# Expert weights of a mixture layer picked from SBUF by registers instead of gathered from memory

## The reference

```python
x = x + _layernorm(_L0_attn_ref(_layernorm(x), ...))   # windowed attention, a recurrence over the tokens
x = x + _layernorm(_L0_ffn_ref(_layernorm(x), ...))    # the second layer
```

```python
attn = softmax(rope(q) @ rope(k).T / sqrt(8)); x1 = layernorm(x + (attn @ v) @ Wo + bo)
gate_probs = softmax(x1 @ Wg + bg)
topk_p, topk_i = top_k(gate_probs, 2); topk_p = topk_p / sum(topk_p)
h = gelu(einsum('bsd,edf->bsef', x1, W1) + b1)         # exact gelu
y = einsum('bsef,efd->bsed', h, W2) + b2
out = layernorm(x1 + einsum('bse,bsed->bsd', comb, y))  # comb: topk_p at the two experts, 0 elsewhere
```

## Time and profile before

| | |
|---|---|
| median of 3 runs (lowest to highest) | 3049.6 us (3047.81 to 3052.29) |
| the profiled execution: its time | 3038.8 us |
| its span, first to last instruction | 3037.1 us |
| PE busy (share) | 1260.7 us (42%) |
| PEld | 573.8 us (19%) |
| DVE | 2243.1 us (74%) |
| ACT | 1239.5 us (41%) |
| POOL | 380.9 us (13%), 495 instructions |
| mean granted TensorE clock | 0.664 of full speed |
| moved by DMA | 104.36 MB, 42.48 of them by the software queue (GpSimd's) |

### The profile page before, as it was taken

How to read it: one execution, slowest core, us unless ns; L and a number is a source line. 1 busy time by engine, 2 the same in 40 slices (tenths; PEclk the granted TensorE clock), 3 DMA queues, 4 the chain that set the end, 5 groups by cost and what they waited for, 6 DMA issues and landing times. The chain is left out here.

```text
span 3037.1 us, 37267 instructions
## 1 busy us (share of the span) xinstructions
PE 1260.7 (42%) x7320; PEld 573.8 (19%) x7320; DVE 2243.1 (74%) x15166; ACT 1239.5 (41%) x3176; POOL 380.9 (13%) x495
## 2 busy tenths in 40 slices
PE   2101101001001001010148785877758777578687
PEld 1000000000000000000011122333213322134255
DVE  6999999999999999998669973645655456554232
ACT  2333333333333333333515652555535554455532
POOL 0000000000000000000101104222043120312111
PEclk8555555555555555555569985878769787688788
DMA  4000000000000000000340202142122321222200
GB/s 100 1 1 1 1 1 1 1 1 1 1 1 1 1 1 1 1 1 3 70 90 18 64 18 76 46 125 61 27 84 75 106 52 21 84 70 66 83 15 8
DMA packets 91680, 104.36 MB, mean 34 GB/s; under 512 B 10350, under 2 KB 66456, under 8 KB 91448
## 3 DMA queue, kind: packets, MB, share of 16 engines
q1 hardware_dynamic: 77336, 59.49, 7.9%
q0 software_dynamic: 14112, 42.48, 4.6%
HBM read 73.04 MB, written 30.67 MB: 34 GB/s over the span
## 5 line engine op out<-in xcount | busy, mean ns | idle before, releaser
L1269 DVE TENSOR_REDUCE nm_half<-pair 128x2 f32<-128x1024 f32 x512 | 618.1, 1221 | 374.0 <-PE pair L1519 268.0
L1166 ACT ACTIVATE pt<-pair 128x1024 f32<-128x1024 f32 x512 | 512.5, 1024 | 523.7 <-PE pair L1529 424.1
L207 ACT ACTIVATE ex<-row,nmax 128x65 f32<-128x65 f32 x960 | 336.0, 350 | 923.5 <-DVE nmax L309 837.8
L267 DVE SCALAR_TENSOR_TENSOR junk<-ex,tab 128x65 f32<-128x65 f32 x2850 | 620.6, 219 | 1.4 <-issue 0.2
L370 PE MATMUL p_s<-tab,bdg 128*128 128x32 f32 x120 | 31.8, 406 | 829.7 <-DVE tab L272 829.7
L1495 PE MATMUL p_o<-pt,va 128*9 128x512 f32 x2048 | 312.1, 683 | 11.1 <-DVE o_sb L1298 5.3
L1519 PE MATMUL pair<-ks,qs 48*128 48x512 bf16 x1024 | 226.5, 440 | 179.1 <-ACT pt L1166 113.8
L272 DVE TENSOR_TENSOR tab<-raw,rz 128x1 f32<-128x1 f32 (+1 forms) x1890 | 285.8, 151 | 3.2 <-issue 1.1
L301 DVE SCALAR_TENSOR_TENSOR junk<-ex,rz,row 128x65 f32<-128x65 f32 x930 | 265.3, 285 | 3.0 <-issue 2.7
L1529 PE MATMUL pair<-qs,ks 50*128 50x512 bf16 x1024 | 223.4, 435 | 62.6 <-DVE nm_half L1269 34.7
L267 DVE DVE_READ_ACCUMULATOR junk<-ex,tab 128x1 f32 x2850 | 235.0, 82 | 0.3
(11 more groups left out here) (257 smaller groups left out, 2049.9 us busy)
## 6 DMA issues: line engine op xcount, KB each, us to landing
parts_dram<-parts SPq DMA_DIRECT2D x48, 256.0 KB
qs<-parts_dram SPq DMA_DIRECT2D x32, 192.0 KB, 4.7
ks<-parts_dram SPq DMA_DIRECT2D x32, 192.0 KB, 5.3
hid<-xs_dram SPq DMA_DIRECT2D x15, 256.0 KB
ys_dram<-hid SPq DMA_DIRECT2D x15, 256.0 KB
h_dram<-f SPq DMA_DIRECT2D x20, 128.0 KB, 2.5
x<-in_x SPq DMA_DIRECT2D x4, 512.0 KB, 8.5
w_dram<-in_W SPq DMA_DIRECT2D x8, 256.0 KB
```

The source lines that it names most:

```text
L207: nc.scalar.activation(ex[:, r % 2, :], row[:, r % 2, 1:], ACT.Exp, bias=nmax[:, r % 2:r % 2 + 1], accum_out=z[:, r % 2:r % 2 + 1]).then_i ...
L267: nc.vector.scalar_tensor_tensor(junk[:, g, :], ex[:, k, :], 1.0, tab[:, g, r:r + ROW], ALU.mult, ALU.mult, accum_out=raw[:, g:g + 1]).the ...
L1166: nc.scalar.activation(pt[:, kt % 2, :, tokens(t)], pair[fill.pair][:, :, :], ACT.Exp, scale=SCALE).then_inc(s_exp, 1)
L1269: nc.vector.reduce_max(nm_half[:, t, hp % 2, :, q], pair[fill.pair][:, :, :], AX.X, negate=True)\
```

## The change

W1 and W2 are loaded once, whole, in the first layer, and stay in SBUF; the copy of W2 in DRAM, the gathers (WG) and the reload (WL) go. A new step WC, due five units ahead of a group, lets GpSimd read the expert of each tile into a register and copy that expert's W1 into `w1`, a single buffer of four tiles in the memory of `yg`. It waits until the first expert product has used the group before (for the first group: until B2 is done with that memory). At the start of a group TensorE reads the same numbers into registers of its own; the product by W2 takes its operand at an address made from the register. `sel`, `upper` and `ones` of the rank products become bf16 (they hold 0, 1 and sums that fit).

```diff
+    pairs += [(w["W1"][:, :, :], io["W1"].rearrange("e d f -> d e f"))]
+    pairs += [(w["W2"][:, e, :, :], io["W2"][e].rearrange("(c p) d -> p c d", p=P)) for e in range(E)]
...
-         (2, 1): [("WG", j) for j in range(SLOTS)], (7, 2): [("YG",)]}
+         (7, 2): [("YG",)]}
...
+            if u + 5 in GROUP_AT:
+                due.insert(0, ("WC", GROUP_AT.index(u + 5)))
             if u + 3 in GROUP_AT:
                 due.insert(0, ("XS", GROUP_AT.index(u + 3)))
-            if u - 4 in GROUP_AT:
-                g = GROUP_AT.index(u - 4) + 2
-                due += [("WG", j) for j in in_group(g)]
...
-            if last and (hp, kt) == (7, 4):
-                due.append(("WL",))
...
-        sel, pw = sb("sel", [P, QT, E]), sb("pw", [P, 2, QT, E])
+        sel, pw = sb("sel", [P, QT, E], BF16), sb("pw", [P, 2, QT, E])
-        upper, ones = sb("upper", [P, P]), sb("ones_pp", [P, P])
+        upper, ones = sb("upper", [P, P], BF16), sb("ones_pp", [P, P], BF16)
...
+        w1 = yg[:, :, :, :].rearrange("p k q d -> p (k q d)").rearrange("p (j i) -> p j i", j=GROUP)
...
+                elif name == "WC":
+                    g = x[1]
+                    pool.wait_ge(s_experts, s)
+                    pool.sem_inc(s_pace_pool, 1)
+                    if g == 0:
+                        taken(pool, at["B2", 1])
+                        pool.sem_inc(s_pace_pool, 1)
+                    else:
+                        pool.wait_ge(s_hs, 2 * NG * (s - 1) + 2 * g)
+                        pool.sem_inc(s_pace_pool, 1)
+                    for j in in_group(g):
+                        e = pool.value_load(expert_u[0:1, j:j + 1], min_val=0, max_val=E - 1)
+                        nc.gpsimd.tensor_copy(w1[:, j % GROUP, :], w["W1"][:, bass.ds(e, 1), :].rearrange("p e i -> p (e i)"))\
+                            .then_inc(s_w1, 1)
...
-                    then(nc.vector.tensor_scalar(row_f[:, :], expert_t[:, :], float(P), parted[:, :], ALU.mult, ALU.add))
+                    nc.vector.tensor_copy(expert_u[:, :], expert_t[:, :]).then_inc(s_experts, 1)
...
                     g = tiles[0] // GROUP
+                    if x[1] % 2 == 0:
+                        pe.wait_ge(s_experts, s)
+                        for j in in_group(g):
+                            chosen[j] = pe.value_load(expert_u[0:1, j:j + 1], min_val=0, max_val=E - 1)
                     taken(pe, at["XS", g])
+                    pe.wait_ge(s_w1, NT * (s - 1) + tiles[-1] + 1)
                     emptied(s, fill)
                     for j in tiles:
-                        pe.wait_ge(s_wg[j % SLOTS], fetches(s, j))
                         for f in range(FC):
-                            ins = nc.tensor.matmul(pair[fill.pair][:, j % 2, tile(f)], w["W1"][:, j % SLOTS, tile(f)],
+                            ins = nc.tensor.matmul(pair[fill.pair][:, j % 2, tile(f)],
+                                                   w1[:, j % GROUP, tile(f)],
                                                    xst[:, g % 2, tile(j % GROUP)], start=True, stop=True)
...
-                                               w["W2"][:, j % SLOTS, f, :], start=f == 0, stop=f == FC - 1)
+                                               w["W2"][:, bass.ds(chosen[j], 1), f, :].rearrange("p e d -> p (e d)"), start=f == 0, stop=f == FC - 1)
```

More of the change, by code:

```diff
@@ L32 @@
 NG = -(-NT // GROUP)
-SLOTS = 2 * GROUP
 SCALE = 1.0 / float(np.sqrt(HD))
@@ L128, in _ @@
             loaded = load_constants(sp, w, io, s_weights)
[L130 to L133, removed]
+            xs_dram, _ = moe_dram
             sp.wait_ge(s_stacks, 2)
@@ L140, in _ @@
                              stacks["ones"][:, :].unsqueeze(1).broadcast_to((2, HP, T))).then_inc(s_weights, 16)
-            sp.wait_ge(s_weights, loaded + 32 + 16 * (E + 1))
+            sp.wait_ge(s_weights, loaded + 32 + 16)
         @block.gpsimd
@@ L858, in second_layer @@
         xr, xa2, acc = sb("xr", [P, QT, D]), sb("xa", [P, 2, QT, D]), sb("acc", [P, QT, D])
-        sel, pw = sb("sel", [P, QT, E]), sb("pw", [P, 2, QT, E])
+        sel, pw = sb("sel", [P, QT, E], BF16), sb("pw", [P, 2, QT, E])
         wk = sb("wk", [P, 2, 2, QT])
-        upper, ones = sb("upper", [P, P]), sb("ones_pp", [P, P])
-        lower, steps8, tiles_at, parted = sb("lower", [P, E, E]), sb("steps8", [P, QT]), sb("tiles_at", [P, NT]), sb("parted", [P, 1])
+        upper, ones = sb("upper", [P, P], BF16), sb("ones_pp", [P, P], BF16)
+        lower, steps8, tiles_at = sb("lower", [P, E, E]), sb("steps8", [P, QT]), sb("tiles_at", [P, NT])
         cmp8, tiles_of, upto, base = sb("cmp8", [P, E, E]), sb("tiles_of", [P, E]), sb("upto", [P, E]), sb("base", [P, E])
@@ L866, in second_layer @@
         before_t, expert_t = sb("before_t", [P, NT, E]), sb("expert_t", [P, NT])
-        row_f, row_u = sb("row_f", [P, NT]), sb("row_u", [P, NT], U32)
+        row_f, expert_u = sb("row_f", [P, NT]), sb("expert_u", [P, NT], U32)
         bias_t = sb("bias_t", [P, NT, FC])
         yg = sb("yg", [P, 2, QT, D])
+        w1 = yg[:, :, :, :].rearrange("p k q d -> p (k q d)").rearrange("p (j i) -> p j i", j=GROUP)
         part = yg[:, 0, :, :].rearrange("p (t q) d -> p t q d", t=2)
@@ L880, in second_layer @@
         hq = hq.rearrange("p (q d) -> p q d", q=QT)
-        xs_dram, ys_dram, w2_dram = moe_dram
+        xs_dram, ys_dram = moe_dram
         xt = aot
@@ L913, in second_layer @@
             sem(n) for n in ("s_gate", "s_gexp", "s_comb", "s_sum", "s_added", "s_fin", "s_out"))
-        s_sel, s_place, s_slots, s_rows, s_bias = (
-            sem(n) for n in ("s_sel", "s_place", "s_slots", "s_rows", "s_bias"))
-        s_sent, s_fetched, s_mixed, s_dense = sem("s_sent"), sem("s_fetched"), sem("s_mixed"), sem("s_dense")
+        s_sel, s_place, s_slots, s_experts, s_bias = (
+            sem(n) for n in ("s_sel", "s_place", "s_slots", "s_experts", "s_bias"))
+        s_sent, s_fetched, s_mixed = sem("s_sent"), sem("s_fetched"), sem("s_mixed")
         s_xs, s_ys = [sem(f"s_xs{i}") for i in range(2)], [sem(f"s_ys{i}") for i in range(2)]
-        s_wg = [sem(f"s_wg{i}") for i in range(SLOTS)]
+        s_w1 = sem("s_w1")
         s_hs, s_gs = sem("s_hs"), sem("s_gs")
@@ L938, in norm_index @@
             return NORMS.index((s, k))
-        def fetches(s, j):
-            return 32 * (len(range(j % SLOTS, NT, SLOTS)) * (s - 1) + j // SLOTS + 1)
         def group_loads(s, g):
@@ L1057, in step @@
                         .then_inc(s_ys[g % 2], 16)
[L1058 to L1063, removed]
             passes(sp, step)
@@ L1075, in _ @@
                            allow_small_or_imprecise_dtypes=True).then_inc(s_iota, 1)
-            nc.gpsimd.iota(parted[:, :], [[1, 1]], base=0, channel_multiplier=1,
-                           allow_small_or_imprecise_dtypes=True).then_inc(s_iota, 1)
             nc.gpsimd.memset(ones[:, :], 1.0).then_inc(s_iota, 1)
@@ L1080, in _ @@
             nc.gpsimd.memset(lower[:, :, :], 1.0).then_inc(s_iota, 1)
-            pool.wait_ge(s_iota, 7)
+            pool.wait_ge(s_iota, 6)
             nc.gpsimd.affine_select(out=upper[:, :], in_=upper[:, :], compare_op=ALU.is_ge, fill=0.0, base=-1,
@@ L1119, in step @@
                                 half_of(xa2, s)[:, q, :], None).then_inc(s_sent, 16)
[L1120 to L1125, removed]
-                        pool.sem_inc(s_pace_pool, 1)
[L1127 to L1133, removed]
+                elif name == "WC":
[4 more added lines that the diff above has]
+                        taken(pool, at["B2", 1])
+                        pool.sem_inc(s_pace_pool, 1)
+                    else:
[5 more added lines that the diff above has]
+                            .then_inc(s_w1, 1)
                 elif name == "YG":
@@ L1455, in step @@
                             dve.sem_inc(s_pace, 1)
-                    nc.vector.tensor_copy(row_u[:, :], row_f[:, :]).then_inc(s_rows, 1)
                     then(nc.vector.tensor_tensor(before_t[:, :, :], expert_t[:, :].unsqueeze(2).broadcast_to((P, NT, E)), tiled,
@@ L1473, in _ @@
             placings = [0]
-            dve.wait_ge(s_iota, 9)
+            dve.wait_ge(s_iota, 8)
             passes(dve, step)
@@ L1478, in _ @@
         def _(pe):
-            at = {}
+            at, chosen = {}, {}
             def emptied(s, fill):
@@ L1550, in step @@
                         taken(pe, at["XT", 1])
-                        pe.wait_ge(s_dense, 32)
                     emptied(s, fill)
@@ L1567, in step @@
                     pe.wait_ge(s_sel, s)
-                    pe.wait_ge(s_iota, 9)
+                    pe.wait_ge(s_iota, 8)
                     flat = sel[:, :, :].rearrange("p q e -> p (q e)")
@@ L1653, in program @@
     parts_dram = nc.dram_tensor("parts_dram", (2, H, PARTS * HD, T), BF16).ap()
-    moe_dram = (nc.dram_tensor("xs_dram", (NT, P, D), F32).ap(), nc.dram_tensor("ys_dram", (NT, P, D), F32).ap(),
-                nc.dram_tensor("w2_dram", (E * P, FC * D), F32).ap())
```

(1 more changed line is left out.)

## The result

The changed kernel takes 2925.0 us (median of 4 runs, 2918.6 to 2933.0), beside 3048.7 us of the kernel before on the same chip (3045.7 to 3052.3): a ratio of 0.9595, 95% interval [0.9569, 0.9621], 124 us less. I had said 93 less, between 38 and 152.

The account below looks back on a forecast made before the run. Second layer: TensorE's chain, broken by stalls in GpSimd's indirect-transfer bursts. Sum 90 + 20 + 14 - 27 - 7 + 3 = 93 us less than 3038.8, plus 10.8 to reach the runs' median: 2956 us, range 2898 to 3012.

Parts of the forecast that it names:

- Gathers gone: Second layer: removing 138 weight gathers and the final reload ends stalls without work, 90 us less, bounds 50 to 115.
- the clock: TensorE after stalls: it no longer restarts at the low 1.2 GHz level, 20 us less, between 5 and 30.
- GpSimd's relief: GpSimd no longer issues gathers, so VectorE's rotation waits less for its split of q and k: 3 us less.
- rival 1: Engines stall for a reason of their own, not the gathers: 17 us slower, 3067 us; chance 8%.
- Rank products: Ranking on TensorE: 16 products per batch in bf16 instead of f32, 14 us less in three batches, bounds 10 and 17.
- Register loads: Start of 18 expert groups on TensorE: loading expert numbers loses 1.5 us each, 27 us more, bounds 0 and 178.
- addresses: Second expert product on TensorE: 69 steps computing register addresses cost 0.1 us each, 7 us more, between 0 and 25.
- Copies on GpSimd: Four W1 copies per expert group cost nothing while covered, up to 5 us per group otherwise.
- rival 2: Each register load waits a full 2.6 us round trip on TensorE, costing 178 us: 3108 us; chance 7%.
- Rival 3: Stalls move to the remaining scatters and result fetches: only 28 us less, 3022 us; chance 13%.
- Rival 4: Register loads are covered and all stalls gone: 154 us less, 2896 us; chance 10%.

Follow-up runs that it names:

- The plain transfers: Kernel before, each gather replaced by a plain GpSimd transfer of the same 256 KB into the same slot, expert fixed: 2919.1 us, one execution.
- the spread scatters: Changed kernel, each batch's 16 scatters issued singly behind successive exponentials, fetches one or two per exponential: 2921.3 us, ratio 0.9622.
- the version without registers: Changed kernel without TensorE's 69 register loads; the second expert product reads W2 of expert j mod 8 at a constant address: 2901.2 us, ratio 0.9555.
- the run with plain tokens: Changed kernel with its 48 scatters and 48 fetches replaced by plain GpSimd transfers of the same bytes: 2868.3 us, one execution.
- small gathers: Kernel without gathers, all 138 put back at a quarter of their size, 128 rows of 512 bytes: 3042.5 us, one execution.
- the version with W2 copied: Changed kernel, but GpSimd also copies W2 of each group's tiles and TensorE loads no register; everything computed: 2897.2 us, ratio 0.9539.

## Why the prediction was right, and where it was off

*Gathers gone, 90, with the clock, 20, and GpSimd's relief, 3.* Measured together, 120 (114 to 133), against 113: their sum was sized well, a little low. It came from the chain's links without work, taken one by one, and from no mechanism, so it could come out although the mechanism was wrong. How the 120 divides was not tested: the share that I left for the scatters (3 us in each of three bursts) and for what else may be late (a quarter of 45.8) were guesses, and part of the agreement may be luck. The clock behind the stall is not priced on its own either; behind the scatters it is 0.80 now instead of 0.50. The relief did not come at all: VectorE's rotation waits 13.1 us for GpSimd, where it was 12.6.

*The mechanism behind it was wrong.* I inferred that engines fetch their instructions late while a burst is in the DMA rings. The plain transfers fill the same rings with the same packets, and nobody stops. The trace of the kernel before speaks against it too. Instructions come in packets of their own on two queues named instruction. The DMA view of 1861.4 to 1882.7, all of ScalarE's long stall and its end, has none of them:

```profile
q0 software_dynamic: 1201, 3.93, 62.1%
q1 hardware_dynamic: 886, 0.44, 7.1%
```

What ScalarE did there stands in the chain, between two pieces in which nothing known released it:

```profile
1881.30 0.02 ACTq L1164
1881.31 1.37 another core or an unknown queue
1882.68 0.02 issue
1882.71 1.03 ACT pt L1166
```

L1164 is an increment of a semaphore that ScalarE's sequencer makes between two waits. It comes 20 us late, when the burst is over; the changed kernel has the same picture at 2425.01. TensorE, whose steps of this layer have no such increments, is never named with a remote wait after 1380 us. But VectorE's step of a maximum (L1269) has none either, only a wait and the reduction, and it stood for 17.02 us; so the increments alone don't tell the held engines from the others. That semaphores pass slowly while GpSimd handles indirect transfers in close succession would fit; it is argued, not shown, and no run here tells it from another cause inside GpSimd's handling. The cause of the stalls stays open. It seems that the pause need not be work, since the spread scatters waited idly and left 2.7 of 29 us, but only half of them had a gap.

*The Trainium skill's two rules.* Its page "SBUF — State Buffer", section "Who interferes with whom", says that DMA never contends with a compute engine. I held ScalarE's 21.4 us against it. The runs take that back in part: 328 GB/s of plain transfers left TensorE busy 13.1 of 14 us, which agrees. What stops the engines is not the data but how GpSimd issues them. The rule on instruction fetch ("Runtime: NRT & Kernel Launch", section "Instruction fetch mechanics") is not contradicted by any run here. I had taken both rules as speaking for rival 1, the stalls not being the gathers'; that step was wrong, for they are silent on the form of the transfer.

*Rank products, 14.* Measured 25 (19 to 33). The term was mis-sized: I priced each product by a weight load that stands alone (0.148 us). A load does take 0.104 us, but eight of them take 0.30 us together, and with their products 0.36. They overlap, which my row did not show, and so nearly all of the 7.0 us goes.

*Register loads, 27, and addresses, 7.* Measured together 12 and 17, each give or take 11, against 34. The profile's idle time gives 21 for the loads (35.5 less 14.5; 23 against the version without registers, which has 12.5), and an address is one instruction of 46 ns that TensorE's work covers. The place and the form were right, as was the choice of the end near GpSimd's 0.30 us: four loads add 1.4 us in most groups (2.27 against 0.86). For the loads of a group 1.5 was close, but in seven of the 18 only 0.15 to 0.9 is added, where the group has three tiles or other work was late anyway. The Trainium skill's floor of some 600 ns a load ("DMA: Bandwidth & Descriptors", section "Latency and other measured facts") made an estimate of 34 in the prediction, more than the 21 that the trace shows; the trace's 1.4 us for four loads in a row is less than four times that floor, even less the 0.5 us that I took as covered.

*Copies on GpSimd, nothing.* Right: 0.613 us each where I had 0.610, and nobody waited.

*Together.* 120 and 25, less 12 to 17, are 128 to 133; the change gives 124. All three terms that were off erred to the same side: gathers by 7, rank products by 11, registers by 17 to 22, 35 to 40 in all. Within the uncertainty of these runs that is the 31 us between 93 and 124.

*Rivals.* Rival 1 (3067) and rival 2 (3108) fell: the gathers were the cause, and a load costs some 0.35 us, far from the 1.8 from which it decides. Rival 3 (3022) was right that scatters and fetches go on stalling, 76 us of remote waits instead of the 60 I expected, but no stall of the gathers moved there. Rival 4 (2896) needed them gone as well, and the run with plain tokens, 2868, shows what that is worth. I wrote that the range takes in most of rival 4; its lower end, 2898, lies above rival 4's 2896, so it took in half of it at best.

## What to carry to other kernels

Look at how the transfers in a burst are made and how closely they follow each other, before you count their bytes: here a pause of 0.9 us between indirect transfers gave more than removing 36 MB of them. When engines wait for something that the profile doesn't name, try the cheapest experiment on the suspected issuer, a pause or a plain transfer of the same bytes, before rebuilding the data flow. And where TensorE needs data chosen at run time, let an idle engine copy it to a fixed place; TensorE then pays for no register (here 17 us, give or take 11).

## What the runs showed of the hardware

- ScalarE and VectorE stop for long stretches while GpSimd issues indirect transfers 0.30 us apart. The longest wait, 22.1 us, fell into 32 in a row (16 scatters and 16 small gathers) and ended 4 us behind the last one; shorter ones end inside a burst. With 0.15 + 0.89 us between the transfers no such wait is left. Plain transfers from GpSimd's queue, 0.56 us each to issue against 0.95, hold nobody at 328 GB/s. TensorE is not named with such a wait in either form.
- Idle gaps seem to do as well as busy ones: of scatters that were spread out by waits, about half had a gap of 0.6 us or more, and one stall of 2.7 us was left of 29 us.
- Four loads of a register from SBUF held TensorE for 1.4 us, one register address costs 46 ns of its sequencer's time, and a product whose operand has such an address took 275 ns (median) as before.
- Eight bf16 products of 128x128 by 8 columns took 0.36 us with their weight loads; the same eight in f32, sixteen records, took 3.55. The granted clock was 0.50, the 1.2 GHz level, around both, and the version with W2 copied shows 0.36 again. The load of one such operand takes 0.104 us, eight take 0.30.
- 138 copies of 128x512 f32 on GpSimd left VectorE's busy time where it was (2243.3 against 2242.5 us).
